# Causal masks moved from TensorE to VectorE and GpSimd in an attention kernel with mixture-of-experts

## What is computed

```python
q = split_heads(x @ Wq.T + bq); k = ...; v = ...         # 16 heads of 32
q_lr, k_lr = q @ Wq_lsr, k @ Wk_lsr                      # per head
scores = einsum('bhir,bhjr->bhij', q_lr, k_lr) * scale
scores = where(triu(ones, k=1), -inf, scores)            # the causal mask
y = einsum('bhij,bhjd->bhid', softmax(scores), v)
x = layernorm(x + y @ Wo.T + bo)
x = layernorm(x + expert_layer(x))                       # 16 experts, capacity 512
```

## Time and profile before

| | |
|---|---|
| median of 3 runs | 4516.19 us (4515.04 to 4518.01) |
| span of the profiled execution | 4512.1 us, first to last instruction |
| busy share of the span: PE, PEld, DVE, ACT, POOL | 88%, 57%, 53%, 32%, 10% |
| matmuls; DVE instructions; POOL instructions | 22121; 4178; 351 |
| mean granted TensorE clock | 0.936 |

### The profile page before, as it was taken

One profiled execution on the slowest core, in us unless ns is written; L12 is line 12 of the kernel. 1 busy time (PEld: TensorE's weight loads), 2 busy tenths in 40 slices (PEclk: granted clock), 3 DMA queues, 4 the chain that ended last, 5 costly groups with the idle time before them and its releaser, 6 DMA issues. The chain is left out here.

```text
span 4512.1 us, 61594 instructions
## 1 busy us (share of the span) xinstructions
PE 3967.5 (88%) x22121; PEld 2589.9 (57%) x22121; DVE 2384.8 (53%) x4178; ACT 1432.2 (32%) x2018; POOL 470.3 (10%) x351
## 2 busy tenths in 40 slices
PE   5999999999999999999999761499999999999950
PEld 3655455545455555455454330388888888888840
DVE  4354554564554546545645457744454445444537
ACT  0332332332323323323233330233333333333324
POOL 2011010010110110100100100001111001111100
PEclk7999999999999999999999885599999999999985
DMA  4422533324324323343241460233344334433439
GB/s 143 76 76 76 94 90 85 74 78 90 94 76 94 84 70 74 90 99 95 64 93 47 164 183 0 78 118 115 114 122 129 114 114 124 126 114 115 125 112 363
DMA packets 246522, 473.22 MB, mean 105 GB/s; under 512 B 38528, under 2 KB 73344, under 8 KB 241664
## 3 DMA queue, kind: packets, MB, share of 16 engines
q1 hardware_dynamic: 220432, 418.04, 32.8%
q0 software_dynamic: 14336, 34.22, 4.2%
q10 hardware_dynamic: 11520, 17.83, 1.1%
HBM read 278.86 MB, written 89.42 MB: 82 GB/s over the span
## 5 line engine op out<-in xcount | busy, mean ns | idle before, releaser
L729 DVE TENSOR_REDUCE max_slots<-shared_banks 128x1 f32<-128x512 f32 (+3 forms) x1536 | 805.1, 550 | 639.5 <-PE shared_banks L539 541.3
L674 ACT ACTIVATE probs<-scores_t 128x1024 f32<-128x1024 f32 (+3 forms) x768 | 611.6, 810 | 916.7 <-PE scores_t L573 534.3
L1568 PE MATMUL m_ps_h<-m_tokens_t,m_w_parts 128*128 128x512 f32 x3072 | 740.4, 391 | 1.6 <-DVE m_tokens_t L1505 1.6
L1568 PE MATMUL m_ps_y<-m_w_parts,m_hidden_parts 128*128 128x512 f32 x3072 | 737.0, 390 | 4.0 <-DVE m_hidden_parts L1534 3.9
L536 PE MATMUL shared_banks<-k_operands,q_operands 96*128 96x512 f32 (+3 forms) x1536 | 619.9, 432 | 65.2 <-DVE max_slots L729 52.6
L1568 PEld LDWEIGHTS m_ps_y<-m_w_parts,m_hidden_parts 128*128 128x128 f32 x3072 | 575.6, 188 | 128.7 <-issue 9.9
L1568 PEld LDWEIGHTS m_ps_h<-m_tokens_t,m_w_parts 128*128 128x128 f32 x3072 | 575.9, 188 | 120.1 <-issue 2.0
L536 PEld LDWEIGHTS shared_banks<-k_operands,q_operands 96*128 96x128 f32 x1536 | 297.0, 197 | 527.2 <-DVE max_slots L729 346.4
L570 PE MATMUL scores_t<-q_operands,k_operands 128*128 128x512 f32 (+3 forms) x1536 | 509.3, 404 | 20.4 <-ACT probs L674 13.8
L1474 ACT ACTIVATE m_hidden<-m_ps_h,m_b 128x512 f32<-128x512 f32 x256 | 176.6, 690 | 821.9 <-PE m_ps_h L1568 808.7
L1532 DVE CAST m_hidden_parts<-m_hidden 128x512 fp32r<-128x512 f32 x256 | 111.1, 434 | 585.3 <-ACT m_hidden L1474 585.3
(11 more groups left out here) (213 smaller groups left out, 3378.8 us busy)
## 6 DMA issues: line engine op xcount, KB each, us to landing
m_w_raw<-in_w1T SPq DMA_DIRECT2D x64, 1024.0 KB, 5.1
m_w_raw<-in_w2T SPq DMA_DIRECT2D x64, 1024.0 KB, 8.6
q_operands<-natural SPq DMA_DIRECT2D x384, 128.0 KB, 2.5
k_operands<-natural SPq DMA_DIRECT2D x384, 128.0 KB, 2.5
wqk_group<-scratch_wqk SPq DMA_DIRECT2D x32, 1024.0 KB, 7.6
scratch_sums<-zeros_f SPq DMA_DIRECT2D x8, 2064.0 KB, 19.3
f_acc<-scratch_sums SPq DMA_DIRECT2D x16, 1032.0 KB, 9.1
natural<-in_xT SPq DMA_DIRECT2D x8, 2048.0 KB, 7.7
```

Source lines behind the costliest of these rows:

```text
L674: act.activation(probs[:, slot_of(k, pair), :, c0:HALF], st[:, pair, :, c0:HALF], ACT.Exp, scale=SCALE).then_inc(exp_done, 1)
L729: dve.tensor_reduce(mx[:, h, slot:slot + 1], src[:, 0:n], AX.X, ALU.max).then_inc(bank_free[bank], 1)
L1568: mm = pe.matmul(bank, a, b, start=(first and n == 0), stop=(final and n == len(pairs) - 1))
```

## The change

The mask matmuls are gone. For the maxima DVE adds the mask in the pass that takes the row maximum: one `tensor_tensor_reduce` reads the bank and a wide bf16 mask whose last 128 columns hold the triangle, writes the masked scores back to the bank and the maximum to `max_slots`. For the probabilities nothing is masked ahead of the exponential; POOL sets the upper triangle of each diagonal block of `probs` to zero with `affine_select` after ACT has written it, and PE's `values` waits for that (`masked`). The maxima no longer follow a `values` item: its share goes behind the `sums` that follows it. POOL makes the parts of the next x in eight pieces, two at each `values` item of steps 8 to 11 of group 2, where before all eight stood ahead of that group's first step. The rule for DVE's pieces of the inversion is now a function, `pieces_at`, that POOL uses as well.

```diff
         order.append(part)
-        if first <= n < final:
+        if first <= n < final and part[0] != "values":
             share = m * (n + 1 - first) // (final - first)
             order += [("max", g, i) for i in range(done, share)]
...
+        def pieces_at(item, left):
+
+            if ends_half(item):
+                return left
+            if left == 0 or not uses_bank(item):
+                return 0
+            if item[0] == "out":
+                return left if item[1] in (0, 2) else 1
+            return 1 if item[0] != "max" or item[2] % 2 == 0 else 0
+
+        SPLIT_FROM = NE - DC
...
+            def split_x(n, piece):
+
+                c = piece % DC
+                if piece == 0:
+                    await_parts(pool, pool_passed, n - 1, GROUPS - 2)
+                    plain(pool, x_in, 16 * (n + 1), pool_passed)
+                if piece < DC:
                     ins = pool.tensor_copy(xs[:, HI, c, :], nat[:, c, :])
-                ins.then_inc(x_split, 1)
-                pool.wait_ge(x_split, 2 * n + 1)
-                for c in range(DC):
+                else:
+                    if piece == DC:
+                        pool.wait_ge(x_split, 2 * n + 1)
                     ins = pool.tensor_tensor(xs[:, LO, c, :], nat[:, c, :], raw(xs[:, HI, c, :]), ALU.subtract)
-                ins.then_inc(x_split, 1)
+                if c == DC - 1:
+                    ins.then_inc(x_split, 1)
+
+            def mask_probs(b, g, k, pair):
+
+                c0 = steps[k][2]
+                s = (b * GROUPS + g) * NE + k
+                block = probs[:, slot_of(k, pair), :, c0:c0 + P]
+                plain(pool, exp_done, 2 * s + pair + 3, pool_passed)
+                pool.affine_select(out=block, in_=block, compare_op=ALU.is_ge, fill=0.0, base=0,
+                                   pattern=[[0, 2], [1, P]], channel_multiplier=-1).then_inc(masked, 1)
...
-                        if diag:
-                            mm = pe.matmul(out[:, n - P:n], identb[:], mask_q[:], start=False, stop=True)
-                        mm.then_inc(bank_full[bank], 1)
+                        pe.matmul(out[:, 0:n], q_ops[0:MAX_STRIP, buf, h, it * P:(it + 1) * P],
+                                  k_ops[0:MAX_STRIP, buf, h, k0:k0 + n], start=True, stop=True
+                                  ).then_inc(bank_full[bank], 1)
...
-                    if diag:
-                        mm = pe.matmul(out[:, c0:c0 + P], identb[:], mask_k[:], start=False, stop=True)
...
-                pe.wait_ge(exp_done, 2 * s + 4)
+                if diagonal[k]:
+                    pe.wait_ge(masked, (b * GROUPS + g) * N_DIAG + masked_through(k))
+                else:
+                    pe.wait_ge(exp_done, 2 * s + 4)
...
-                        dve.wait_ge(bank_full[bank], off + turn + 1)
-                        dve.tensor_reduce(mx[:, h, slot:slot + 1], src[:, 0:n], AX.X, ALU.max
-                                          ).then_inc(bank_free[bank], 1)
+                        if k0 + n == (it + 1) * P:
+                            plain(dve, bank_full[bank], off + turn + 1, dve_passed)
+                            dve.tensor_tensor_reduce(out=src[:, 0:n], in0=src[:, 0:n], in1=mask[:, HALF - n:HALF],
+                                                     scale=1.0, scalar=LOWEST, op0=ALU.add, op1=ALU.max,
+                                                     accum_out=mx[:, h, slot:slot + 1]).then_inc(bank_free[bank], 1)
```

More of the change, by code:

```diff
@@ L28 @@
 MASKED = -(2.0 ** 120)
+LOWEST = -3.0e38
 ACC = D + 4
@@ L309, in build_attention, with masked_through @@
         assert PROB_BUFS == 4 and (2 * NE) % PROB_BUFS == 0
+        diagonal = [j * P >= hh * HALF for hh, j, _ in steps]
+        N_DIAG = 2 * sum(diagonal)
+        def masked_through(k):
+            return 2 * sum(diagonal[:k + 1])
         def ends_half(item):
             return item[0] == "sums" and steps[item[2]][1] == 4 * steps[item[2]][0] + 3
+        def pieces_at(item, left):
[7 more added lines that the diff above has]
+        SPLIT_FROM = NE - DC
         def turns(order, base):
@@ L433, in split_x @@
[L433 to L437 removed]
+            pool.affine_select(out=mask[:, HALF - P:], in_=mask[:, HALF - P:], compare_op=ALU.is_ge, fill=MASKED,
+                               base=0, pattern=[[-1, P]], channel_multiplier=1).then_inc(consts, 1)
+            def split_x(n, piece):
[4 more added lines that the diff above has]
+                if piece < DC:
@@ L454, in run @@
                 order, _, _ = scope(b)
+                more = not (isinstance(b, int) and b == NB - 1)
+                left, half = 0, None
                 for item in order:
[L456 to L459, removed]
+                    left -= pieces_at(item, left)
+                    if half is not None and left == 0:
+                        normalise(b, *half)
+                        half = None
+                    if ends_half(item):
+                        half, left = (item[1], steps[item[2]][0]), DEN_PIECES - 1
+                    if item[0] == "scores" and diagonal[item[2]]:
+                        mask_probs(b, *item[1:])
+                    if more and item[0] == "values" and item[1] == GROUPS - 2 and item[2] >= SPLIT_FROM:
+                        for piece in range(2):
+                            split_x(b + 1, 2 * (item[2] - SPLIT_FROM) + piece)
                     if item[0] != "out":
@@ L567, in scores @@
                     h = 2 * pair + q
-                    out = st[:, pair, q, :]
-                    diag = j * P >= hh * HALF
-                    mm = pe.matmul(out[:, c0:HALF], k_ops[:, buf, h, j * P:(j + 1) * P],
-                                   q_ops[:, buf, h, hh * HALF + c0:(hh + 1) * HALF], start=True, stop=not diag)
-                    if diag:
-                        mm = pe.matmul(out[:, c0:c0 + P], identb[:], mask_k[:], start=False, stop=True)
+                    mm = pe.matmul(st[:, pair, q, c0:HALF], k_ops[:, buf, h, j * P:(j + 1) * P],
+                                   q_ops[:, buf, h, hh * HALF + c0:(hh + 1) * HALF], start=True, stop=True)
                 mm.then_inc(st_full, 1)
@@ L694, in run @@
                     kind = item[0]
+                    for _ in range(pieces_at(item, len(pieces))):
+                        invert(b, *pieces.pop(0))
                     if ends_half(item):
-                        while pieces:
-                            invert(b, *pieces.pop(0))
                         n = 2 * (b * GROUPS + item[1]) + steps[item[2]][0]
@@ L708, in run @@
                     src = shared[:, bank, :]
-                    if pieces and (kind != "max" or item[2] % 2 == 0):
-                        invert(b, *pieces.pop(0))
-                    while pieces and kind == "out" and item[1] in (0, 2):
-                        invert(b, *pieces.pop(0))
                     if kind == "proj":
```

31 lines of the change are left out of this document (11 added, 20 removed).

## The result

The changed kernel takes 4703.82 us (median of four runs, 4693.11 to 4722.98) where the kernel before takes 4515.61: a ratio of 1.0431, 95% interval 1.041 to 1.0451, 188 us more.

A forecast was written before the change was run, and what follows sets the result against it. PE was taken to set the pace, with gains only where DVE is not next in line. Walk 53, last group -2, split 60, clock 30 and 18 summed to +159 us on 4516: 4675 us, range 4590 to 4790.

The forecast's parts named there:

- What bounds it: Attention: PE sets the pace, but work taken off it is gained only where DVE is not next in line.
- The group's walk: One attention group stepped through by its waits for banks: +1.7 us per group, +53 us over 31 groups.
- values 0 to 2: Group's first steps, without maxima: eight score masks go between values 0 and values 2, -0.8 us.
- the wait behind the sums of step 3: PE stands for a bank while DVE copies and inverts pieces: 2.6 us where it was 0.96.
- Values 3 to 4: Stretch from values 3 to values 4: 6.3 us instead of 5.53, counted as +0.8 per group.
- The other steps: Six remaining steps of a group: between 0 and +0.3 us each, +0.8 together, from longer bursts of maxima.
- The clock: TensorE at 1.2 GHz after waits: +30 us at steps 4 and 5 in 19 more groups, +18 behind the split.
- The split: POOL's subtractions for x end late; PE stands 8.5 us before group 3's projection 0, seven times: +60 us.
- The new pass: DVE's mask and maximum in one pass: +0.03 us each over the plain reduction, 0.1 more before starting when idle.
- Half rate: Rival: DVE's new pass runs at half rate, adding 150 us, for 4825 us; chance 8%.
- TensorE stays the bound: Rival: DVE keeps up, the 174 us of masks are gained, and the kernel takes 4420 us; chance 9%.
- The split is hidden: Rival: POOL's subtractions are not exposed before group 3's projection, so 78 us go, for 4597 us; chance 12%.

The follow-up runs named there:

- both_back: The changed kernel with maxima between the products again and the split of x two steps earlier; 4535.80 us, 1.0060 of the kernel before.
- all_spread: both_back with the normalisation behind the bias of output tile 2 again and the inversion pieces ahead of every fourth maximum; 4427.71 us, 0.9809 of before.
- masks_twice: both_back with the 2048 mask matmuls issued on TensorE as well, so masks are made in both places; 4605.14 us, 1.0209 of before.
- maxima_only: The kernel before with only the masks of the maxima moved into DVE's pass; 4528.65 us, 1.0038 of before.
- scores_only: both_back with the maxima's mask matmul and plain reduction put back, POOL's select kept for the score masks; 4505.48 us, 0.9980 of before.
- scores_norm: scores_only with a batch's last normalisation behind the bias of output tile 2 again in POOL's queue; 4461.93 us, 0.9891 of before.
- order_alone: The kernel before with only the new order of maxima, none between values and sums; 4572.54 us, 1.0139 of before.

## Why the prediction was right, point by point

4675 us was forecast and 4704 measured, in the range and on the side that had 0.87. The parts, each by the run that takes it out: order 103, split 51, the two instructions in POOL's queue 48; together 202 where 188 were measured, so that some 14 are left, by difference, as what the removal of the masks gives back. In the prediction's terms: its walk and clock, removal included, forecast 81 and come to 89; its split forecast 78 and comes to 51; 48 it did not have. The runs are not strictly additive (the split is worth 65 us by medians once the order is back, 51 without), so these are shares to within some 15 us.

- *What bounds it* held: work was taken off TensorE and its waits for DVE grew from 48.8 to 194.5 us (L753 and L758 together).
- *The group's walk.* At the full clock: values 0 to 2 4.82 us (4.9 forecast), 2 to 3 4.74 (4.8), 5 to 6 5.29 (5.4), the wait behind the sums of step 3 2.37 (2.6). Values 3 to 4 is in no group at the full clock throughout; it takes 6.46 to 7.09, least where the clock falls last (6.3 forecast). The other steps, +0.8 together in the walk, came to about 0 up to values 10. So the group is some 0.6 us longer at the full clock, an estimate from these steps with 6.47 for values 3 to 4, not 1.7: 20 us, not 53.
- *The clock*, forecast +30, was undersized. The falls behind the wait came about as told, in 31 groups, which is the forecast's 12 and 19 more. What the term left out is that the clock also falls at steps 8 to 10, 43 times over the whole attention. 375 us more at the lower level, where the same work takes up to twice as long, are up to 188 us. An estimate of what they did cost: of the 188 us measured, 20 are the walk's, 45 the stands for the split (7 of 6.4) and 23 the output stage's, which leaves 100 for the clock, where 30 and 18 were forecast. The walk too dear and the clock too cheap all but cancel, and that is luck. What makes the clock fall at step 10 no run tells apart. The falls there go from 16 in both_back to 8 in all_spread, and there are none in any kernel that still issues masks on TensorE, masks_twice, maxima_only and scores_only among them.
- *The split*: +60 and +18 forecast, 51 to 65 measured. The stall is 6.4 us, not 8.5: POOL ends 9.8 us after the last exponential as reckoned (10.2), but PE comes 3.5 us after it, not 1.7, since it waits 1.10 for the row maxima and has a lower clock. The projection behind it takes 5.32 us, 2.3 more than in rows 7, as forecast (2.5).
- *The missed term.* One edit in POOL's part of the diff, the normalisation that follows the count of pieces instead of `t == 2`, was not walked at all: it moves a waiting instruction ahead of one that DVE needs. It is worth 48 us. Without it the kernel takes 4656 us, 19 below the forecast, with it 29 above, both in the range. The total came out as near as it did because errors of several tens of microseconds have opposite signs.
- *The new pass* cost +0.02 us (taken +0.03). *Half rate* (8%) is out: 0.711 us for a bank in PSUM and a bf16 tile. The rule of the Trainium skill ("Vector Engine (DVE) Microarchitecture Reference", Points that are easy to get wrong) speaks of the instruction format `S2S2D2_STT` with two SBUF sources that are not bf16. The trace lists this pass as a custom instruction, so it agrees with the rule as read in the prediction but doesn't show that the rule covers the pass; a case in which it would bite was not run.
- *TensorE stays the bound* (9%) is out: the same masks moved without order, split and the third place are worth about nothing (both_back less its output stage, a subtraction and no run). In the traces waits and clock take what TensorE was relieved of. *The split is hidden* (12%) is out for the change, but true for the same split without selects in front of it.

## What to carry to other kernels

Walk every reordered pair on an in-order queue, also one that a refactoring swaps in passing: a waiting instruction put ahead of a ready one cost 48 us here, and the place of an instruction in the program says nothing about its time; what stands ahead of it does. Of the two moves only one paid by itself: with the old order and POOL's two instructions put back, score masks by POOL's select make the kernel 1.1% faster (scores_norm), while masks of the maxima in DVE's pass make it 0.4% slower (maxima_only). Before taking work off TensorE, remove the waits at which it stands: one of 1.11 us or more costs itself, and in most groups the clock behind it. With the inversion spread over the maxima and the two instructions of POOL in their old order, the kernel without masks on TensorE is 1.9% faster than before, without these two edits 0.6% slower. Spreading the inversion in the kernel before was not tried, so how much of this it would give alone stays open.

## What the hardware showed that I had not expected

- The falls of the clock at steps 3 and 4 go with the length of one wait, whatever masks TensorE still issues. With 0.13 and 0.47 us none of the 31 groups with maxima has one, with 0.96 (three runs and before) 12 to 16, with 0.99 19, with 1.11 (three runs) 20 to 24, with 2.18 and 2.35 30 or 31. order_alone, with every mask on TensorE, has 31.
- At step 10 it is otherwise: the eight kernels that still issue some masks on TensorE have no fall there, the six that issue none have 8 to 30. Why stays open.
- In both_back a wait of 1.12 us behind the sums of step 3 is followed by the lower level in 23 of 32 groups; in all_spread, with 0.15 in its place and 0.47 as the longest up to values 4, in none, though TensorE issues the same matmuls.
- The reading of the accumulator behind the masked pass takes 0.142 us, in rows 5 0.083, yet it starts together with the next pass and costs nothing on DVE when the next pass stands ready.
